# A mixture-of-experts stage on one core: shared expert with stationary weights over 512 tokens, router sigmoid from tanh and silu

## Chip, cores and metric

One core of one Trainium2 chip runs the whole program. The metric is the device time of one execution in microseconds; the kernel before has a median of 911.48 us over 3 runs (911.13 to 911.8).

## What is computed

Two layers over x of 2 x 2048 tokens by 256 channels: attention, a mixture of experts, a time-mixing layer with a scan, a channel-mixing layer. The part that matters here is the mixture of experts on the normalised rows (E = 8 experts, F = 192, top 2):

```python
logits = x @ W_gate_router
scores = jax.nn.sigmoid(logits.astype(jnp.float32))
_, sel = jax.lax.top_k(scores + expert_bias, TOP_K)
top_scores = jnp.take_along_axis(scores, sel, axis=1)
top_scores = top_scores / (top_scores.sum(-1, keepdims=True) + EPS)
shared = jax.nn.silu(x @ Wg_s) * (x @ Wu_s) @ Wd_s
...
out = shared.at[tok].add(routed)
```

All matrix products are made of three passes on values split into a high and a low part (high x high, high x low, low x high), so every operand is converted twice: a copy to the high part (ScalarE, ACT) and a subtraction for the low part (VectorE, DVE).

## The kernel before

The program runs in stages with a barrier after the first: attention (0 to 333 us of the span), then in one block the dense stage (335 to 477), the slots of the routed experts (477 to 632) and the two last layers. The change lies in the dense stage. It takes 8 groups G of 512 tokens (4 tiles of 128). For each group:

- `z_of`, `turn_z`, `h_of`: the rows are normalised (ACT), transposed on TensorE (PE) and scaled to `hf`, 256 channels x 512 tokens, by ACT.
- `logits`: 16 PE matmuls of 8 columns against the router (line 1620); `sigmoid` on ACT (line 1243); `choose` on DVE, 13 small instructions from `sel` (line 1382) to `both` (line 1395), which many semaphore links serialise; `count` on PE (lines 1638, 1640) ranks the tokens; `weigh` and `rank_of` on DVE give weights and row numbers; GpSimd (POOL) scatters the rows to DRAM (line 1148).
- `h_hi`, `h_lo`: the split of `hf` into `hh` and `hl`; `turn_h`, `h_back`: rows transposed back for the scatter.
- The shared expert by tiles of 128 tokens, n = 0 to 31: `up(n)` has the tokens stationary and the gate and up weights moving, 6 matmuls of 384 columns (lines 80 to 82); `silu` (line 1253) and `hidden` (lines 1427, 1428) make the product; `turn` transposes it (lines 1656, 1657), `ht_hi` and `ht_lo` split it (lines 1258, 1434, 1435), `shared_down` multiplies with the down weights, 5 matmuls of 256 columns (lines 1664 to 1668), and `add` adds the tile to x (line 1440).
- `up_weights`, `down_weights`, `low_up_weights`, `low_down_weights`: one routed expert's weights per group are loaded and split.

Each engine goes through an order written out by hand: the loop over G in the blocks of ACT (line 1270 on), DVE (line 1456 on) and PE (line 1680 on). The shared expert of group G-1 is interleaved with the routing of group G. ACT holds one table of functions at a time; sigmoid and silu each bring a table load per group.

After group 7 DVE computes from the counts where the slots of the routed experts lie (lines 1464 to 1506). `fill_at` releases SP's eight fills of the rows behind each expert (line 1071); `tabled`, the fills and the scatters release SP's loads of slots (line 1082), with which the next stage begins.

Of the kernel before, what the change touches and what calls it, by code (L numbers as in the profile page):

```python
# [28 lines left out]
ALU = mybir.AluOpType  # L29
# [11 lines left out]
GT = 4  # L41
# [755 lines left out]
def experts_time_and_channels(nc, k, d):  # L797
# [7 lines left out]
    N1 = GROUPS * GT  # L805
# [6 lines left out]
    with ExitStack() as ctx:  # L812
# [18 lines left out]
        iota_e, iota_i = sl("iota_e", [P, E]), sl("iota_i", [P, P + 32], U32)  # L831
        sig, sel = sl("sig", [P, GT, E]), sl("sel", [P, GT, E])
        best, place = sl("best", [P, GT, 8]), sl("place", [P, GT, 8], U32)
# [21 lines left out]

        late = sb("late", [P, B * KC * D + KC * P + B * D])
        there, order, mine = (late[:, i * E * TPE:(i + 1) * E * TPE].rearrange("p (t e) -> p t e", e=E) for i in range(3))
        spot = late[:, 3 * E * TPE:3 * E * TPE + E + TPE + 2 * E + TPE + 2 + 2 * SLOTS]
# [20 lines left out]
        spare = dense.enter_context(nc.sbuf_tensor("spare", [P, 6 * KC * GW], F32))  # L879
# [3 lines left out]
        raw_gu = part(0, 4 * KC * F).rearrange("p (r c n) -> p r c n", r=2, c=KC)  # L883
        raw_dn = part(2048, 4 * D).rearrange("p (r c n) -> p r c n", r=2, c=2)
        gated_dn = part(3072, 2 * B * D).rearrange("p (b c n) -> p b c n", b=B, c=2)
        z = part(4096, GT * D).rearrange("p (t n) -> p t n", t=GT)
        hf = part(5120, KC * GW).rearrange("p (c n) -> p c n", c=KC)
# [61 lines left out]
        tp, dp, lg, bk = (bank[:, i] for i in range(4, 8))  # L949
        wgu_in, wdn_in = ([sem(f"m_{n}_in{i}") for i in range(2)] for n in ("wgu", "wdn"))  # L950
# [5 lines left out]
                 "ranked hb_ready hb_done gu_ready silu_done hid_done ht_ready ht_hi ht_lo d_done x_added "  # L956
                 "fill_at filled spread slots_known tabled z_turned y_done tagged tokened named "
# [93 lines left out]
        def _(sp):  # L1051
# [11 lines left out]
            weights(0, d["wg_s"], d["wu_s"], d["wd_s"])  # L1063
# [37 lines left out]
        def _(pool):  # L1101
# [54 lines left out]
            pool.wait_ge(s["tabled"], 1)  # L1156
            for c in range(KC):
                last = g_.tensor_scalar_mul(lnb[:, c], plain[:], col(k, "ln_b", c))
# [38 lines left out]
        def _(act):  # L1197
# [36 lines left out]
            def h_hi(G):  # L1234
                act.wait_ge(s["h_f"], (G + 1) * KC)
                need(act, s["gu_ready"], (G - 1) * GT)
# [18 lines left out]
            def ht_hi(n):  # L1255
                act.wait_ge(s["ht_ready"], n + 1)
                need(act, s["d_done"], n - 1)
                a_.copy(hth[:, n % 2], tp[:, 0:2 * P]).then_inc(s["ht_hi"], 1)
# [6 lines left out]
            z_of(1)  # L1265
            sigmoid(0)
            up_weights(1, 0)
            down_weights(1, 0)
            h_back(0, 0)
            h_back(0, 1)  # L1270
            for G in range(1, GROUPS + 1):
                n = (G - 1) * GT
                if G < GROUPS:
                    h_of(G)
                silu(n)
                if G < GROUPS:
                    sigmoid(G)
                    h_hi(G)
                if n:
                    ht_hi(n - 1)  # L1280
                silu(n + 1)
                ht_hi(n)
                if G < GROUPS:
                    h_back(G, 0)
                if G + 1 < GROUPS:
                    z_of(G + 1)
                silu(n + 2)
                ht_hi(n + 1)
                if G < GROUPS:
                    h_back(G, 1)  # L1290
                silu(n + 3)
                ht_hi(n + 2)
                if G < GROUPS:
                    up_weights(G + 1, G)
                    down_weights(G + 1, G)
            ht_hi(N1 - 1)

            def slot_hi(p):
                act.wait_ge(s["z_turned"], of_pair(p)[-1] + 1)
                need(act, s["gu_ready"], N1 + 2 * p - 2 if p >= 2 else 0)  # L1300
                a_.copy(pair_of(hh, p), pair_in_bank(p)).then_inc(s["hi_h"], 1)

            def pair_ht_hi(p):
                w = len(of_pair(p))
                act.wait_ge(s["ht_ready"], N1 + p + 1)
                act.wait_ge(s["d_done"], N1 + 2 * p)
                a_.copy(hth[:, 0:w], tp[:, 0:w * 2 * P].rearrange("p (r f) -> p r f", r=w)).then_inc(s["ht_hi"], 1)

            def y_of(j):
                act.wait_ge(s["d_done"], N1 + j + 1)  # L1310
# [14 lines left out]
            for p in range(PAIRS + 1):  # L1325
# [4 lines left out]
                for j in of_pair(p):  # L1330
                    silu(N1 + j)
# [11 lines left out]
                if p == PAIRS - 1:  # L1343
                    edge_hi(act, 0)
                    act.wait_ge(s["gu_ready"], N1 + SLOTS)
# [6 lines left out]
        def _(v):  # L1352
# [20 lines left out]
            def h_lo(G):  # L1373
                need(v, s["gu_ready"], (G - 1) * GT)
# [47 lines left out]
            def hidden(n):  # L1422
                v.wait_ge(s["silu_done"], n + 1)
                need(v, s["ht_ready"], n - 1 if n < N1 else N1 + (n - N1) // 2)
# [6 lines left out]
            def ht_lo(n):  # L1431
                v.wait_ge(s["ht_hi"], n + 1)
                need(v, s["d_done"], n - 1)
                vec.tensor_tensor(htl[:, n % 2], tp[:, 0:P], hth[:, n % 2, 0:P], ALU.subtract)
# [1021 lines left out]
```

## Time and profile before

| | before |
|---|---|
| median of 3 runs | 911.48 us |
| the profiled execution | 915.1 us, of it 913.4 us span |
| PE busy over the span, mean granted clock | 838.2 us (92%), 0.958 |
| dense stage, from the first load to the first slot on PE | 335 to 477 us |
| busy from 402 to 416 us (14 us) | PE 12.09, DVE 11.66, ACT 10.43, POOL 7.20 us |

### The profile page before, as it was taken

The numbers are of one execution on the slowest core, as the hardware profiler recorded it, in microseconds if no ns is written. First come the engines' busy times: TensorE is split into PE (matmuls) and PEld (weight loads), VectorE is DVE, ScalarE is ACT, GpSimd is POOL, SyncE is SP. The second block draws the span as 40 slices with busy tenths as digits, with TensorE's granted clock in tenths as the row PEclk, the third lists the DMA queues.
The fourth block names the chain that finished last, engine by engine and source line by source line (L and its number), as shares of the span: only waits on it lengthen the run. The fifth ranks groups of instructions, "written<-read, shape, count | busy, mean of one in ns | idle before, by whom it ended". The sixth has DMA issues, their size and how long they took to land.

```text
span 913.4 us, 16937 instructions
## 1 busy us (share of the span) xinstructions
PE 838.2 (92%) x5115; PEld 748.6 (82%) x5115; DVE 653.9 (72%) x1917; ACT 474.4 (52%) x1006; POOL 378.7 (41%) x427
## 2 busy tenths in 40 slices
PE   7999999999999978888869999999789899988997
PEld 6879998988999867777749999999567788876776
DVE  3665677655567767787865675577677998878986
ACT  1544343243434348878625666466254344449883
POOL 2542200267000023555542444475678886323330
PEclk9899999989999987999988999999799999989999
DMA  9200000000000023433235445343411200000112
GB/s 304 106 1 2 1 1 1 1 1 1 1 1 1 1 56 114 122 106 122 79 118 148 133 117 172 95 125 119 127 47 47 92 2 1 1 1 24 47 47 70
DMA packets 48072, 58.31 MB, mean 64 GB/s; under 512 B 5616, under 2 KB 43121, under 8 KB 47985
## 3 DMA queue, kind: packets, MB, share of 16 engines
q1 hardware_dynamic: 39856, 38.85, 14.6%
q0 software_dynamic: 6480, 16.92, 5.1%
q10 hardware_dynamic: 1648, 1.46, 0.5%
q8 instruction: 45, 0.74, 0.3%
q14 instruction: 43, 0.34, 0.1%
HBM read 34.91 MB, written 23.22 MB: 64 GB/s over the span
## 4 chain that ended last, share of the span: by engine, by line
PE 31%; DVE 16%; issue 7%; ACT 4%; POOL 2%; SPq 1%; DMA 1%; DVEq 0%; ACTq 0%; POOLq 0%
PE bank L80 7%; PE bank L81 6%; PE bank L82 6%; PE bank L1721 2%; PE bank L1729 2%; PE bank L1620 1%; DVE xm L2110 1%; PE bank L1737 1%; DVE st L2046 1%; PE bank L1738 1%; PE bank L1741 1%; PE bank L1739 1%; PE bank L1740 1%; DVE hth L1435 1%; DMA row_tiles<-region 1%
## 5 line engine op out<-in xcount | busy, mean ns | idle before, releaser
L374 ACT CAST pth<-tp 128x512 fp32r<-128x512 f32 (+3 forms) x80 | 41.7, 525 | 128.8 <-PE tp L735 127.5
L1164 POOL DMA_INDIRECT results<-row_tiles,idu x71 | 70.0, 986 | 91.1 <-ACT row_tiles L1313 76.7
L1148 POOL DMA_INDIRECT region<-row_tiles,posu x64 | 66.3, 1036 | 59.8 <-DVE posu L1419 42.7
L559 DVE TENSOR_TENSOR ptl<-tp,pth 128x512 fp32r<-128x512 f32 (+3 forms) x80 | 48.3, 608 | 54.6 <-ACT pth L374 54.5
L80 PE MATMUL cx<-vh,pth 128*128 128x256 f32 x272 | 80.7, 297 | 1.4 <-DVE ptl L559 1.2
L82 PE MATMUL cx<-vh,ptl 128*128 128x256 f32 x272 | 76.9, 283 | 0.0
L81 PE MATMUL cx<-vl,pth 128*128 128x256 f32 x272 | 76.9, 283 | 0.0
L80 PE MATMUL sc<-hh,ph 128*128 128x512 f32 (+3 forms) x160 | 61.2, 382 | 0.3
L82 PE MATMUL sc<-hh,pl 128*128 128x512 f32 (+3 forms) x160 | 58.3, 364 | 0.0
L81 PE MATMUL sc<-hl,ph 128*128 128x512 f32 (+3 forms) x160 | 58.1, 363 | 0.0
L365 ACT ACTIVATE prob<-sc,nmx 128x512 f32<-128x512 f32 (+3 forms) x80 | 49.4, 628 | 14.0 <-DVE nmx L530 14.0
L1253 ACT ACTIVATE act_g<-bank 128x192 f32<-128x192 f32 x103 | 34.1, 331 | 41.4 <-PE bank L82 40.5
L80 PEld LDWEIGHTS cx<-vh,pth 128*128 128x128 f32 x272 | 51.8, 190 | 3.0 <-DVE ptl L559 2.3
L80 PE MATMUL bank<-h3h,weights 128*128 128x512 f32 x128 | 52.3, 408 | 1.2 <-DVE h3l L1030 1.2
L263 POOL TENSOR_SCALAR z<-x,mv,rstd 128x256 f32<-128x256 f32 x24 | 30.3, 1273 | 54.6 <-PE tp L623 53.9
L81 PEld LDWEIGHTS cx<-vl,pth 128*128 128x128 f32 x272 | 51.9, 191 | 0.7
L80 PE MATMUL bank<-guh,hh 128*128 x142 | 52.1, 367 | 0.0
L82 PEld LDWEIGHTS cx<-vh,ptl 128*128 128x128 f32 x272 | 51.8, 190 | 0.0
L82 PE MATMUL bank<-h3h,weights 128*128 128x512 f32 x128 | 51.6, 403 | 0.0
L81 PE MATMUL bank<-h3l,weights 128*128 128x512 f32 x128 | 51.4, 402 | 0.0
L735 PE MATMUL tp<-ident,prob 128*128 128x128 f32 x272 | 43.6, 276 | 5.9 <-ACT prob L365 5.9
L81 PE MATMUL bank<-gul,hh 128*128 x142 | 48.8, 344 | 0.0
(430 smaller groups left out, 2802.1 us busy)
## 6 DMA issues: line engine op xcount, KB each, us to landing
row_tiles<-region SPq DMA_DIRECT2D x71, 130.0 KB, 2.4
pairs_a<-results SPq DMA_DIRECT2D x10, 512.0 KB, 4.4
x<-in_x SPq DMA_DIRECT2D x8, 512.0 KB, 8.6
out<-x SPq DMA_DIRECT2D x8, 512.0 KB, 2.9
pairs_b<-results SPq DMA_DIRECT2D x6, 512.0 KB, 4.3
early<-in_wmod SPq DMA_DIRECT2D x1, 1536.0 KB, 7.9
spare<-in_wg SPq DMA_DIRECT2D x8, 192.0 KB
spare<-in_wu SPq DMA_DIRECT2D x8, 192.0 KB
```

The lines of the kernel that those rows point to most:

```text
L80: eng.matmul(out, lh, rh, start=first, stop=False)
L81: eng.matmul(out, lh, rl, start=False, stop=False)
L82: return eng.matmul(out, ll, rh, start=False, stop=last)
L263: g_.tensor_scalar(z[:, G % 2, j], k.x[:, t], mv[:, t, 0:1], rstd[:, t:t + 1], ALU.subtract, ALU.mult).then_inc(s["z_done"], 1)
L365: a_.activation(prob[:, u % 2, o:o + w], sc[:, score_bank(m), 0:w], ACT.Exp, bias=nmx[:, t:t + 1], scale=1.0 / 16, accum_out=rsc[:, t, ch: ...
L374: a_.copy(pth[:, m % 2, 0:w], tp[:, m % 2, 0:w]).then_inc(s["pt_hi"], 1)
L559: vec.tensor_tensor(ptl[:, m % 2, 0:w], tp[:, m % 2, 0:w], pth[:, m % 2, 0:w], ALU.subtract).then_inc(s["pt_lo"], 1)
L735: last = nc.tensor.transpose(tp[:, m % 2, j * P:(j + 1) * P], prob[:, UNIT_OF[m] % 2, a:a + P], k.ident[:])
L1148: g_.indirect_dma_start(region, bass.IndirectOffsetOnAxis(ap=posu[:, c, t:t + 1], axis=0), hb[:, G % HB, j], None).then_inc(scattered[G % ...
L1164: g_.indirect_dma_start(results, bass.IndirectOffsetOnAxis(ap=idu[:, j % 8:j % 8 + 1], axis=0), y[:, j % YR, 0:D], None, bounds_check=KS * ...
L1253: a_.activation(act_g[:, n % 2], gu[:, n % 2, 0:F], ACT.Silu).then_inc(s["silu_done"], 1)
L1721: last = nc.tensor.transpose(zp[:, 0, o:o + P], gt[:, j % GR, c * P:(c + 1) * P], k.ident[:])
```

## The change

The shared expert goes by groups. `up_shared(G, m)` has 128 columns of the weights stationary and 512 tokens moving, 6 matmuls each; the weights are laid out on the host as gate 0 to 127, up 0 to 127, then gate and up 128 to 191 together, so m = 0, 1, 2 give three banks with the hidden channels on partitions. No transposes of the product are left. `shared_down` takes two tiles at a time into the one bank `dp`, 10 matmuls, and `add` adds two tiles. The router's sigmoid is made of tanh (0.5 tanh(x/2) + 0.5) and, where relu(-0.5 - x) is above zero, silu(x)/x. The orders of ACT, DVE and PE are written anew.

On ACT:

```diff
             def sigmoid(G):
                 act.wait_ge(s["logits"], G + 1)
                 need(act, s["route"], G)
-                a_.activation(sig[:].rearrange("p t e -> p (t e)"), bk[:, 0:GT * E], ACT.Sigmoid).then_inc(s["sig_done"], 1)
+                a_.copy(flat(logit), bk[:, 0:GT * E])
+                a_.activation(flat(silu_l), bk[:, 0:GT * E], ACT.Silu)
+                a_.activation(flat(sel), bk[:, 0:GT * E], ACT.Relu, bias=k.mhalf[:, 0:1], scale=-1.0)
+                a_.activation(flat(sig), bk[:, 0:GT * E], ACT.Tanh, scale=0.5).then_inc(s["sig_done"], 1)
...
+            def gate_wide(G):
+                act.wait_ge(s["up_ready"], 3 * G + 1)
...
+                a_.activation(wide, up_bank[0], ACT.Silu).then_inc(s["gated"], 1)
+            def gate_narrow(G):
+                act.wait_ge(s["up_ready"], 3 * G + 2)
+                a_.activation(narrow[0:F - P], up_bank[2][0:F - P], ACT.Silu).then_inc(s["gated"], 1)
+            def hid_hi(G):
+                act.wait_ge(s["multiplied"], 2 * G + 1)
...
+                a_.copy(h2[0:F - P], narrow[0:F - P]).then_inc(s["hid_hi"], 1)
+                act.wait_ge(s["multiplied"], 2 * G + 2)
+                a_.copy(h1h, wide).then_inc(s["hid_hi"], 1)
...
+            for G in range(GROUPS):
+                sigmoid(G)
                 if G + 1 < GROUPS:
                     z_of(G + 1)
+                h_back(G, 0)
+                h_back(G, 1)
+                gate_wide(G)
+                up_weights(G + 1, G)
+                gate_narrow(G)
+                if G + 1 < GROUPS:
+                    h_of(G + 1)
+                hid_hi(G)
+                if G + 1 < GROUPS:
+                    h_hi(G + 1)
+                down_weights(G + 1, G)
```

On DVE (behind the loop stand the table of slots, `add(7, 0)`, `add(7, 1)` and the copies that set `tabled`):

```diff
             def choose(G):
                 v.wait_ge(s["sig_done"], G + 1)
+                vec.reciprocal(logit[:], logit[:])
+                c_.link(vec.tensor_scalar(sig[:], sig[:], 0.5, 0.5, ALU.mult, ALU.add))
+                c_.link(vec.tensor_tensor(silu_l[:], silu_l[:], logit[:], ALU.mult))
+                c_.link(vec.copy_predicated(sig[:], sel[:].bitcast(U32), silu_l[:]))
...
+            def multiply_narrow(G):
+                v.wait_ge(s["gated"], 2 * G + 2)
+                vec.tensor_tensor(narrow[0:F - P], narrow[0:F - P], up_bank[2][F - P:P], ALU.mult).then_inc(s["multiplied"], 1)
+            def multiply_wide(G):
+                v.wait_ge(s["up_ready"], 3 * G + 3)
+                vec.tensor_tensor(wide, wide, up_bank[1], ALU.mult).then_inc(s["multiplied"], 1)
+            def hid_lo(G):
+                v.wait_ge(s["hid_hi"], 2 * G + 1)
+                vec.tensor_tensor(h2[F - P:P], narrow[0:F - P], h2[0:F - P], ALU.subtract).then_inc(s["hid_lo"], 1)
+                v.wait_ge(s["hid_hi"], 2 * G + 2)
+                vec.tensor_tensor(h1l[:], wide, h1h, ALU.subtract).then_inc(s["hid_lo"], 1)
+            def add(G, i):
+                v.wait_ge(s["down_done"], 2 * G + i + 1)
...
+                vec.tensor_tensor(xt, xt, dp, ALU.add).then_inc(s["x_added"], 1)
...
+            for G in range(GROUPS):
+                choose(G)
+                if G:
+                    add(G - 1, 0)
+                weigh(G)
+                rank_of(G)
+                if G:
+                    add(G - 1, 1)
+                if G == GROUPS - 1:
                     v.wait_ge(s["const2"], 2)
                     c_.link(vec.tensor_copy(fillu[:], base[:]))
                     v.sem_inc(s["fill_at"], 1)
+                multiply_narrow(G)
+                multiply_wide(G)
+                low_up_weights(G + 1, G)
+                hid_lo(G)
+                if G + 1 < GROUPS:
+                    h_lo(G + 1)
+                low_down_weights(G + 1, G)
```

On PE:

```diff
+            def up_shared(G, m):
+                for c in range(KC):
+                    last = three(nc.tensor, up_bank[m], gsh[:, c, up_cols(m)], gsl[:, c, up_cols(m)], hh[G % 2][:, c], hl[G % 2][:, c],
+                                 c == 0, c == KC - 1)
+                last.then_inc(s["up_ready"], 1)
+            def shared_down(G, i):
+                pe.wait_ge(s["hid_lo"], 2 * G + 2)
+                need(pe, s["x_added"], 2 * G + i)
...
+            for G in range(GROUPS):
+                logits(G)
...
+                if G:
+                    shared_down(G - 1, 0)
+                turn_h(G, 0)
+                if G:
+                    shared_down(G - 1, 1)
+                turn_h(G, 1)
+                pe.wait_ge(s["lo_h"], (G + 1) * KC)
...
+                up_shared(G, 0)
...
+                count(G)
...
+                up_shared(G, 2)
+                if G + 1 < GROUPS:
+                    turn_z(G + 1)
+                need(pe, s["multiplied"], 2 * G)
+                up_shared(G, 1)
+            shared_down(GROUPS - 1, 0)
...
+            shared_down(GROUPS - 1, 1)
```

Before, PE and ACT also turned z of group 1 ahead of everything else of group 1; now `turn_z(1)` stands behind `up_shared(0, 2)`. The slots keep their work and count their semaphores from zero; buffers move.

## Rows read from the trace of the kernel before

**Rows 1.** The page: busy time, share of the span and instructions of each engine.

```profile
PE 838.2 (92%) x5115; PEld 748.6 (82%) x5115; DVE 653.9 (72%) x1917; ACT 474.4 (52%) x1006; POOL 378.7 (41%) x427
```

**Rows 2.** Timeline of PE, dense stage: start us, us, instruction, idle time and releaser.

```profile
422.08 0.60 PE L1632 MATMUL bank<-ident,spare 128*128 128x128 f32 x4
...
422.99 0.42 PE L80 MATMUL bank<-gsh,hh 128*128 128x384 f32 x1
...
425.52 0.36 PE L1664 MATMUL bank<-dsh,hth 128*128 128x256 f32 x1
...
426.20 1.04 PE L1612 MATMUL bank<-ident,spare 128*128 128x128 f32 x8
427.00 0.42 PE L80 MATMUL bank<-gsh,hh2b 128*128 128x384 f32 x1
...
428.54 1.95 PE L1620 MATMUL bank<-router,spare 128*128 128x8 f32 x16 [0.25 <-ACT spare L1231]
...
443.93 1.95 PE L1620 MATMUL bank<-router,spare 128*128 128x8 f32 x16 [0.25 <-ACT spare L1231]
```

**Rows 3.** Timeline of DVE, one group of the dense stage.

```profile
416.68 0.29 DVE L1434 TENSOR_TENSOR htl<-bank,hth 128x128 fp32r<-128x128 f32 x1 [2.15 <-issue]
...
417.64 0.18 DVE L1382 TENSOR_TENSOR sel<-sig,rows 128x32 f32<-128x32 f32 x1
...
419.83 0.27 DVE L1427 TENSOR_TENSOR hid<-act_g,bank 128x128 f32<-128x128 f32 x1
...
422.74 1.29 DVE L1377 TENSOR_TENSOR hl2b<-spare,hh2b 128x512 fp32r<-128x512 f32 x2
...
427.90 0.96 DVE L1360 TENSOR_TENSOR gul<-spare,guh 128x768 fp32r<-128x768 f32 x1
...
429.44 0.27 DVE L1427 TENSOR_TENSOR hid<-act_g,bank 128x128 f32<-128x128 f32 x1
```

**Rows 4.** Timeline of ACT, dense stage.

```profile
342.65 2.08 ACT L1220 ACTIVATE spare<-x,nmr,rstd 128x256 f32<-128x256 f32 x4
...
348.48 0.58 ACT L1248 COPY row_tiles<-bank 128x512 f32<-128x512 f32 x1 [1.01 <-PE bank L1632]
...
415.24 1.13 ACT L1238 CAST hh2b<-spare 128x512 fp32r<-128x512 f32 x2
...
416.66 1.28 ACT L1253 ACT_TABLE_LOAD   x1
```

**Rows 5.** Timeline of PE in the attention stage: matmuls of 512 columns, eleven in sequence.

```profile
305.22 0.39 PE L81 MATMUL sc<-hl,ph 128*128 128x512 f32 x1
...
307.51 0.39 PE L82 MATMUL sc<-hh,pl 128*128 128x512 f32 x1
```

**Rows 6.** The same timeline at the start of the dense stage: the router's matmuls of groups 0 and 1.

```profile
340.19 3.56 PE L1620 MATMUL bank<-router,spare 128*128 128x8 f32 x16 [0.96 <-ACT spare L1231]
...
352.00 3.56 PE L1620 MATMUL bank<-router,spare 128*128 128x8 f32 x16 [2.23 <-ACT spare L1231]
```

**Rows 7.** Timeline of DVE and SP at the end of the dense stage.

```profile
458.46 0.17 DVE L1419 CAST posu<-posf 128x8 uint32<-128x8 f32 x1
...
461.51 9.55 SPq L1071 DMA_DIRECT2D region<-zero  x8
473.27 14.10 SPq L1082 DMA_DIRECT2D row_tiles<-region  x9
...
479.02 0.69 DVE L1521 TENSOR_TENSOR hl<-bank,hh 128x512 fp32r<-128x512 f32 x1 [3.61 <-ACT hh L1301]
```

**Rows 8.** Busy by stretch, PE alone: us, PE busy (instructions), granted clock, DMA share, GB/s.

```profile
449.00:450.00 1.00, 1.00 (x6) 0.50 0.37 133
...
461.00:462.00 1.00, 0.00 (x0) 1.00 0.37 133
...
476.00:477.00 1.00, 0.00 (x0) 1.00 0.13 34
...
478.00:479.00 1.00, 0.37 (x2) 0.50 0.42 88
```

More of the change, by code:

```diff
@@ L1264, in _ @@
             down_weights(0, SH)
[L1265 to L1284, printed above, removed]
+            for G in range(GROUPS):
+                sigmoid(G)
                 if G + 1 < GROUPS:
                     z_of(G + 1)
[L1287 to L1296, printed above, removed]
+                h_back(G, 0)
[9 more added lines that the diff above has]
+                down_weights(G + 1, G)
             def slot_hi(p):
                 act.wait_ge(s["z_turned"], of_pair(p)[-1] + 1)
-                need(act, s["gu_ready"], N1 + 2 * p - 2 if p >= 2 else 0)
+                need(act, s["gu_ready"], 2 * p - 2 if p >= 2 else 0)
                 a_.copy(pair_of(hh, p), pair_in_bank(p)).then_inc(s["hi_h"], 1)
@@ L1330, in _ @@
                 for j in of_pair(p):
-                    silu(N1 + j)
+                    silu(j)
                 if 1 <= p < PAIRS - 1:
@@ L1453, in _ @@
             v.wait_ge(s["tokened"], 1)
-            choose(0)
-            weigh(0)
-            low_up_weights(1, 0)
-            low_down_weights(1, 0)
-            for G in range(1, GROUPS + 1):
-                n = (G - 1) * GT
-                if G == 1:
-                    rank_of(0)
-                if G == GROUPS:
+            for G in range(GROUPS):
[7 more added lines that the diff above has]
+                if G == GROUPS - 1:
                     v.wait_ge(s["const2"], 2)
@@ L1495, in _ @@
-                if G < GROUPS:
-                    weigh(G)
-                    h_lo(G)
-                hidden(n + 2)
-                ht_lo(n + 1)
-                add(n)
-                if G == GROUPS:
-                    v.wait_ge(s["slots_known"], 1)
-                    vec.tensor_copy(exf[:], lg[:, 0:SLOTS])
-                    vec.tensor_copy(exu[:], lg[:, 0:SLOTS])
-                    c_.link(vec.tensor_scalar(colf[:], lg[:, SLOTS:2 * SLOTS], -1.0, float(USED), ALU.mult, ALU.add))
-                    vec.tensor_copy(colu[:], colf[:]).then_inc(s["tabled"], 1)
@@ new lines, in _ @@
+                low_down_weights(G + 1, G)
+            c_.link(vec.tensor_tensor(n_e[:], base[:], ebase[:], ALU.subtract))
+            c_.link(vec.tensor_tensor(there, n_e[:].unsqueeze(1).to_broadcast([P, TPE, E]),
+                                      m128[:].unsqueeze(2).to_broadcast([P, TPE, E]), ALU.is_gt))
+            flat = lambda a: a.rearrange("p t e -> p (t e)")
+            c_.link(vec.tensor_tensor_scan(flat(order), plain[:, 0:1].to_broadcast([P, E * TPE]), flat(there), 0.0, ALU.mult, ALU.add))
@@ new lines, in _ @@
+            c_.link(vec.tensor_tensor(order, order, there, ALU.mult))
+            c_.link(vec.tensor_scalar(mine, order, own[:, 0:1], None, ALU.is_equal))
+            vec.tensor_reduce(in_e, mine.rearrange("p t e -> p e t"), AX.X, ALU.add)
+            c_.link(vec.tensor_reduce(in_t, mine, AX.X, ALU.add))
+            vec.tensor_tensor(terms[:, 0:E], in_e, iota_e[:], ALU.mult)
+            vec.tensor_tensor(terms[:, E:2 * E], in_e, by_e[:], ALU.mult)
+            c_.link(vec.tensor_tensor(terms[:, 2 * E:], in_t, by_t[:], ALU.mult))
@@ L1562, in _ @@
                 for j in of_pair(p):
-                    hidden(N1 + j)
+                    hidden(j)
                 if p == PAIRS - 1:
```

218 lines of the change are left out of this document (84 added, 134 removed).

## The prediction, made blind

> **What bounds the kernel now.** I read the page first: PE is busy 92% of the span and no other engine comes near [rows 1]. That is a mean over stages with different limits, so the stage that changes has to be read by itself, in the timelines of its engines. The router's matmuls mark the groups: they start at 428.54 and 443.93, so a group takes 15.39 us [rows 2]; from group 1 at 352.00 [rows 6] to group 7 at 443.93 it is 91.93 us for six, 15.32 each. Inside a group PE is not the limit. DVE waits 2.15 us once per group [rows 3], and the ACT timeline shows why: the low part of a tile waits for ACT's high part, and ACT goes through its queue of splits and Silu's table load of 1.28 us [rows 4]. So the period is a ring of waits from engine to engine, and removed work pays only where it lies on the ring that the new order makes. The chance to go wrong here is to add up the removed work.
>
> **What goes.** Per group the change removes from PE eight transposes; up falls from 24 matmuls of 384 columns to 18 of 512, which cost (307.51 - 305.22)/10 = 0.229 us each [rows 5]. From ACT go two table loads of 1.28, from DVE some 2 us in all (fewer, wider instructions, against four small ones more for the sigmoid). All of that is real, and I cost it at nothing: none of it sets the new period, as the next part shows. The cover is the ring itself.
>
> **The new ring.** PE's second `shared_down(G-1, 1)` waits for `add(G-1, 0)`, since both halves share one bank; on DVE that add stands behind `choose(G)`. On PE, everything that makes the next hidden product (`turn_h`, `up_shared` 0, `count`, `up_shared` 2, `turn_z`, `up_shared` 1) stands behind that `shared_down`. And on DVE, `choose(G+1)` stands behind `multiply_wide(G)`, which needs `up_shared` 1. So a DVE run and a PE run follow one another and do not overlap:
>
> DVE run, with 0.1 us off each duration because the next instruction starts that much earlier: `multiply_wide`, 512 columns from the matmul's bank, 0.69 [rows 7], taken 0.61. Low parts of a routed expert's weights, from 427.90 to 429.44: 1.54 [rows 3]. `hid_lo`, two of 512 columns, as the pair of `h_lo`, 1.29: taken 1.20; `h_lo` 1.20 [rows 3]. The four new small instructions of `choose`: the trace has none of their kind; from below four that hide behind each other, some 0.4, from above four linked ones as long as `sel`'s 0.18 [rows 3] with a link each, some 1.1; I take 0.8, nearer the linked end, since three of them carry links. The rest of `choose`, 417.64 to 419.83: 2.19 [rows 3]. `add` of 512 columns to its end: 0.69 [rows 7]. Sum 8.23.
>
> PE run: `shared_down` with ten matmuls; five with the lead of the first take 0.68, from 425.52 to 426.20 [rows 2], and five more 0.60: 1.28. `turn_h` and `count`, from 422.08 to 422.99: 0.91 [rows 2]. Three times six matmuls of 512 columns, 6 x 0.229 and 0.08 of lead: 1.45 each, 4.35. `turn_z`, 426.20 to 427.00: 0.80 [rows 2]. The last matmul's end, 0.39 less 0.23: 0.16 [rows 5]. Sum 7.50. Two hand-overs, an estimate of 0.2 together. **Ring at full clock: 8.23 + 7.50 + 0.2 = 15.93 us**, 0.6 more than 15.32.
>
> ACT stays off it: in the DVE run it has to deliver the high part of the wide product, `h_hi` (1.13 for the pair [rows 4]), the down weights and the four small functions, some 3.5 us ending before `choose` is reached, 4.6 us into the run. The routing's tail (`weigh`, `rank_of`, the second `add`) runs on DVE during the PE run, some 3.2 us of 7.5. SP's and POOL's queues keep their order and counts; a weight load has a whole group of slack.
>
> **The clock.** In the new order PE has only `logits`, ten matmuls and four transposes to do during the 8.2 us of the DVE run, and then stands for some 3.7 us until the add. Before, the group had no such hole and the router's matmuls ran at 1.95 [rows 2]. Two rows bear on it. At 461 to 462 PE did nothing and the granted clock stayed 1.00 [rows 8]; at 476 to 477 PE did nothing either, and by 478 to 479 it was 0.50; at 449 to 450, right behind a busy group, it was 0.50 with PE busy throughout [rows 8]. So the clock falls after thin work, not surely after one short hole. I expect it to fall in nearly every group and to come back within the PE run. The price: from below 0 (no fall), from above 7.5 (the whole run at half clock). The nearest rows are the same 16 matmuls at 3.56 [rows 6] and 1.95 [rows 2], 1.6 lost; some of the slow stretch lies in the wait, where it costs nothing, so I take 1.3. **Ring with it: 17.2 us.**
>
> The Trainium skill, "TensorE: Matmul & The Clock Gate", section "Why this matters for your kernels", says to leave no gaps between bursts of matmuls, or the clock goes back to its lower level. By that rule the fall comes in every group and the ring is 17.2; by the row at 461 alone it would not come and the ring is 15.93. No run here shows this order yet.
>
> **The start.** Group 0's logits end at 340.19 + 3.56 = 343.75 [rows 6]. Sigmoid with one table load, 1.9: 345.7. `z_of(1)` comes next on ACT, 2.0, then `h_back`, 0.58 [rows 4]: 348.25. `turn_h` at half clock 0.7, `up_shared` 0 at half clock 2.6: 351.5. From there at full clock `count` 0.56, `up_shared` 2 1.45, `turn_z` 0.80, `up_shared` 1 1.45: **group 1 starts at 355.8 instead of 352.00**, 3.8 later (at half clock to the end, 360.1). Before, group 1's z was turned while ACT and DVE worked at group 0's routing.
>
> **The end.** Group 7's logits start at 355.8 + 6 x 17.2 = 459.0, against 443.93: 15.1 later. Its row numbers came 458.63 - 443.93 = 14.7 after that [rows 7, 2]. Now: 0.1 and the DVE run 8.23, a hand-over 0.15, `shared_down` 1.28, `turn_h` 0.35, `up_shared` 1.45, `count` with its end 0.75, `rank_of` 1.0: 13.3, and 1.3 for the clock: 14.6. From there the fills led to the first slot load, 461.51 to 473.27 [rows 7]. They come up to 0.9 sooner, since an add of 0.61 stands ahead of `fill_at` where weights of 1.54 stood. But `tabled` now comes behind the whole product of group 7 and a PE round trip, 13 to 14 us after the row numbers, just where the fills' end is. I count 0.4 of the 0.9. Sum: 15.1 - 0.1 - 0.4 = **14.6 us later**. The later stages keep their time.
>
> The profiled execution took 915.1 us, 3.6 above the median of the three runs, 911.48. The difference is applied to the median: 911.5 + 14.6 = **926 us**; the profiled execution would be 929.7.
>
> **Rivals.** (A) The clock holds. For it: the idle microsecond at 461 and the steady groups of before. Against it: 478 and 449. Then the ring is 15.93: group 7 starts at 451.4, 7.5 later; row numbers 1.4 earlier relative to that; 0.4 off: 5.7, so 917 us. (B) Faster: the ring is not what I read, and what paces the groups is DVE's wait behind the table load, which goes. Its place is the 2.15 us before the low part [rows 3]; its price is a period of 15.39 - 2.15 = 13.24. Then 3.8 - 6 x 2.08 - 0.4 = -9.1: 902 us. It decides if DVE run and PE run together come under 15.0: 3.8 + 6 x (15.0 - 15.32) - 1.4 - 0.4 = 0. Against it: the wait on the add is written in PE's order, and every long term has its own row. (C) The change doesn't do what it says: tanh and silu do not share a table. Two loads of 1.28 per group remain. The one before tanh delays `choose` by about 0.1, as ACT had 1.1 us in hand; the one before the gate lies in ACT's wait. With 1.3 in group 0 that is some 2 us more than the forecast: 928 us.
>
> **How the numbers follow.** The forecast of 926 has a chance of 0.60, A 0.22, B 0.06, C 0.06; 0.06 is left for a ring near 15.0, where gain and loss cancel. Faster by over 0.2% (about what a measurement of this kernel can tell from no change): B and a little of the last, 0.07. Within 0.2%: 0.06. Slower: the rest, 0.87. The range reaches down to A less its unknowns, 917 - 3, and up to the forecast with about one more us of clock loss in each of the seven periods, 926 + 8: 914 to 934. The fully slow PE run and B lie outside.
>
> **What would show it.** Right: router matmuls 16 to 18.5 us apart; one wait of PE over 3 us per group, ended by the add; a DVE that hardly waits from `multiply_wide` to `add`; `up_shared` at 0.43 per matmul for part of most groups; no table load but the first; group 1 starting near 356. Wrong: a period under 15.0; PE's longest wait ended by something other than the add; the clock at 1.00 throughout (then A); a first slot load set by `tabled` by more than a microsecond; or later stages that change their own length.

## The result, and the profile after

The changed kernel takes **934.24 us** (median of four runs, 931.88 to 937.21), the kernel before on the same chip 911.64 (four runs). The ratio is 1.0239, with a 95% interval of 1.0193 to 1.0284: slower, by 22.6 us. The forecast was 926.0 with a range of 914 to 934, so the direction came out, the median lies 0.24 above the upper end, and the sum was 8 us short. The experiments below show whether the mechanism was the one forecast.

The profiled execution took 937.21 us with a span of 935.2, against 915.1 and 913.4 before. The page's busy times, to be read against [rows 1]:

```profile
PE 834.4 (89%) x5003; PEld 746.5 (80%) x5003; DVE 647.3 (69%) x1837; ACT 456.9 (49%) x983; POOL 378.1 (40%) x427
```

Every engine is busy for less time than before, and the span is 21.8 us longer. What grew is waiting, and the view of waits for the stretch from 360 to 486 us says of what (the columns are the sum in us, how often, and the longest):

```profile
PE bank L1670 <- DVE x L1465: 23.1, 7, 3.7
...
PE bank L1670 <- DVE h1l L1459: 9.8, 7, 1.5
```

L1670 is the first matmul of `shared_down`, L1465 the add, L1459 the second half of `hid_lo`. Seven times PE stands 3.3 us for the add, and seven times 1.4 us for the hidden product. Before, in the steady groups from 367 us on, PE's longest wait was 0.8 us, and ahead of the router's matmuls it was 0.25 [rows 2].

One group on DVE, in the timeline (start, duration, instruction, idle time before and its releaser):

```profile
414.85 0.69 DVE L1453 TENSOR_TENSOR spare<-spare,bank 128x512 f32<-128x512 f32 x1 [0.95 <-PE bank L82]
415.45 0.95 DVE L1372 TENSOR_TENSOR gul<-raw_up,guh 128x768 fp32r<-128x768 f32 x1
416.43 0.69 DVE L1457 TENSOR_TENSOR h2t<-spare,h2t 64x512 fp32r<-64x512 f32 x1
417.15 0.69 DVE L1459 TENSOR_TENSOR h1l<-spare,hth 128x512 fp32r<-128x512 f32 x1
417.76 1.29 DVE L1389 TENSOR_TENSOR hl<-spare,hh 128x512 fp32r<-128x512 f32 x2
...
419.63 0.34 DVE L1394 RECIPROCAL logit<-logit 128x32 f32<-128x32 f32 x1
...
420.69 0.19 DVE L1398 TENSOR_TENSOR sel<-sig,rows 128x32 f32<-128x32 f32 x1
...
422.64 0.68 DVE L1465 TENSOR_TENSOR x<-x,bank 128x512 f32<-128x512 f32 x1
```

Nothing after the first row shows an idle time: from `multiply_wide` (L1453) to the end of the add at 423.32 DVE works 8.47 us through. The four new small instructions of `choose` are the stretch from 419.63 to 420.69, 1.06 us here; in the eight groups they take 0.86 to 1.06, and the whole run takes 8.34 to 8.48 in the seven that end in such an add, 8.41 in the mean of the six periods. Then PE, in the same group:

```profile
423.46 0.36 PE L1670 MATMUL bank<-dsh,hth 128*128 128x256 f32 x1 [2.37 <-DVE x L1465]
...
424.48 0.42 PE L1672 MATMUL bank<-dsh,h1l 128*128 128x256 f32 x1
...
426.83 0.63 PE L82 MATMUL bank<-hh,gsl 128*128 128x512 f32 x1
427.25 0.57 PE L80 MATMUL bank<-hh,gsh 128*128 128x512 f32 x1
...
432.10 0.40 PE L82 MATMUL bank<-hh,gsl 128*128 128x512 f32 x1
```

The second `shared_down` starts 0.14 us after the add, and PE's run lasts from 423.46 to 432.50, 9.04 us. Its first 256-column matmuls come 0.12 apart, from 424.27 on they come 0.21 apart, and `up_shared` 0 goes at 0.43 a matmul until 427.7; from there on it is 0.23. That is the lower of the two clock levels (1.2 GHz) from 424.3 to 427.7. This group is not the usual one in one respect: its first `shared_down` ran slowly too. In the other six groups with two `shared_down` to do, the first ran at full speed, and the slow stretch of the matmuls lies on the second, behind the wait. The timeline of the group from 378.30:

```profile
382.36 0.28 PE L1671 MATMUL bank<-dsl,hth 128*128 128x256 f32 x1
382.48 0.28 PE L1672 MATMUL bank<-dsh,h1l 128*128 128x256 f32 x1
...
387.11 0.55 PE L1670 MATMUL bank<-dsh,hth 128*128 128x256 f32 x1 [3.69 <-DVE x L1465]
387.47 0.42 PE L1671 MATMUL bank<-dsl,hth 128*128 128x256 f32 x1
387.68 0.41 PE L1672 MATMUL bank<-dsh,h1l 128*128 128x256 f32 x1
```

The matmuls come 0.12 apart ahead of the wait and 0.21 behind it. In the six periods PE's run takes 8.85 to 10.21 us, 9.19 in the mean. The view by stretch gives the granted clock from one router group to the next (columns: us, then busy time and instructions of PE, PE's weight loads, DVE, ACT and POOL, granted clock, DMA share, GB/s):

```profile
342.60:360.80 18.20, 14.86 (x57) 12.83 (x57) 9.72 (x43) 11.37 (x21) 5.92 (x6) 0.54 0.29 88
360.80:378.30 17.50, 12.53 (x77) 11.28 (x75) 11.49 (x46) 9.06 (x21) 7.22 (x7) 0.90 0.28 91
...
414.70:432.30 17.60, 13.84 (x76) 12.42 (x76) 11.63 (x46) 9.42 (x21) 8.27 (x8) 0.81 0.31 99
...
467.40:483.60 16.20, 11.61 (x61) 10.39 (x61) 10.11 (x44) 5.45 (x13) 6.07 (x6) 0.68 0.16 58
```

Before, the four steady groups from 382.7 to 443.9 ran at 1.00. The router's matmuls now start at 342.55, 360.76, 378.30, 395.79, 414.65, 432.33, 449.90 and 467.36: 18.21 for group 0, then 17.77 as the mean of six, against 15.32 before [rows 2, 6].

With the row numbers (the end of the last `posu`, 483.61) and the first slot load (498.60) the difference of the two spans splits up:

| stretch | before, us | after, us | difference | forecast |
|---|---|---|---|---|
| up to group 0's logits | 340.19 | 342.55 | +2.4 | 0 |
| group 0 to group 1 | 11.81 | 18.21 | +6.4 | +3.8 |
| six periods | 91.93 | 106.60 | +14.7 | +11.3 |
| group 7's logits to its row numbers | 14.70 | 16.25 | +1.6 | -0.1 |
| row numbers to the first slot load | 14.64 | 14.99 | +0.3 | -0.4 |
| the rest | 440.1 | 436.6 | -3.5 | 0 |
| span | 913.4 | 935.2 | +21.8 | +14.6 |

The first and the last line are code that the change leaves alone, but for counts and places of buffers. In the ten traces of the changed kernel and of the experiments group 0's logits start anywhere between 336.10 and 343.65, and the rest after the first slot load takes 435.7 us in e1, 439.9 in e5 and 435.2 in e7, so these two differences are about the scatter of single executions.

### The profile page after: what moved, and what is told of

The parts are those of the page before. It is cut to its first block, busy times and chain, and to the rows that moved or that the text cites. A ratio compares the mean times of both kernels' runs of the same rounds, so it can differ in the third digit from the quotient of the medians.

```text
span 935.2 us, 16461 instructions
## 1 busy us (share of the span) xinstructions
PE 834.4 (89%) x5003; PEld 746.5 (80%) x5003; DVE 647.3 (69%) x1837; ACT 456.9 (49%) x983; POOL 378.1 (40%) x427
## 4 chain that ended last, share of the span: by engine, by line
PE 38%; DVE 16%; issue 5%; POOL 2%; ACT 2%; DMA 0%; SPq 0%; DVEq 0%; ACTq 0%; POOLq 0%
PE bank L80 8%; PE bank L81 8%; PE bank L82 8%; PE bank L1720 2%; PE bank L1728 2%; DVE xm L2109 1%; PE bank L1736 1%; PE bank L1616 1%; PE bank L1737 1%; PE bank L1740 1%; PE bank L1738 1%; PE bank L1739 1%; DVE st L2045 1%; PE bank L1636 1%; DVE gul L1372 1%
## 5 line engine op out<-in xcount | busy, mean ns | idle before, releaser
L82 PE MATMUL bank<-guh,hl 128*128 x142 | 48.8, 343 | 0.0
```

The costliest lines, as they stand in the source:

```text
L82: return eng.matmul(out, ll, rh, start=False, stop=last)
```

## The experiments

Two questions were open: is the ring of the prediction really what sets the pace, and what made it longer than 17.2? The periods of all kernels, worked out from the starts of the router's matmuls in one trace of each:

| kernel | group 1 starts | group 7 starts | mean of six periods | time, us | ratio to before |
|---|---|---|---|---|---|
| before | 352.00 | 443.93 | 15.32 | 911.64 | 1 |
| after | 360.76 | 467.36 | 17.77 | 934.24 | 1.0239 |
| e1 add first | 354.65 | 439.69 | 14.17 | 906.94 | 0.9949 (0.9910 to 0.9988) |
| e2 hole filled | 351.76 | 454.27 | 17.09 | 925.35 | 1.0170 (1.0119 to 1.0221) |
| e3 old sigmoid | 357.58 | 459.54 | 16.99 | 926.68 | 1.0163 (1.0125 to 1.0201) |
| e4 new sigmoid alone | 356.66 | 458.08 | 16.90 | 922.16 | 1.0106 (1.0059 to 1.0154) |
| e5 weights in the wait | 360.83 | 436.08 | 12.54 | 896.69 | 0.9825 (0.9789 to 0.9861) |
| e6 the same, old sigmoid | 357.54 | 438.79 | 13.54 | 902.16 | 0.9875 (0.9831 to 0.9920) |
| e7 start and tail | 351.54 | 429.48 | 12.99 | 893.59 | 0.9804 (0.9765 to 0.9842) |
| e8 Silu loads first | 356.91 | 433.10 | 12.70 | 897.07 | 0.9815 (0.9782 to 0.9848) |
| e9 swap alone | 352.01 | 451.37 | 16.56 | 922.84 | 1.0118 (1.0088 to 1.0147) |

**e1: the add ahead of `choose`.** One line of DVE's order moves.

```diff
-                choose(G)
                 if G:
                     add(G - 1, 0)
+                choose(G)
                 weigh(G)
```

> The changed kernel with one line moved on DVE: the first add of the group before stands ahead of choose instead of behind it. Theory (a ring of a DVE run and a PE run that cannot overlap because PE's second shared_down waits for the add behind choose): shared_down, turn_h and the first up_shared now run beside choose, so the PE run behind choose shrinks by about 1.3 + 0.35 + 1.45 = 3.1 us, the ring at full clock is near 13.3 us instead of 15.9, and the hole that let the clock fall closes; 7 periods of 17.8 become about 13.3 to 13.8, so 900 to 908 us, below the kernel before. Rival (the wait on the add is only where a slow DVE shows): DVE's work per group is unchanged, the period stays above 16 us and the time at 922 to 934.

Measured: 906.94 us, period 14.17 (13.95 from group 3 on). The time is inside what the theory expected, the period a little above it. Moving one instruction past `choose` takes 27 us off and turns the slower kernel into one that beats the kernel before by half a per cent. The other half of the expectation failed: the clock did not come back. It read 0.78 in the first of the six periods and 0.88 in every later one, so the gain does not come from the clock:

```profile
383.90:397.80 13.90, 12.49 (x76) 11.10 (x76) 11.61 (x46) 9.44 (x21) 7.98 (x8) 0.88 0.39 126
```

The timeline of DVE shows what the add waits for now:

```profile
417.47 0.69 DVE L1465 TENSOR_TENSOR x<-x,bank 128x512 f32<-128x512 f32 x1 [0.57 <-PE bank L1674]
418.07 0.35 DVE L1394 RECIPROCAL logit<-logit 128x32 f32<-128x32 f32 x1
```

DVE is early and waits 0.57 for the first `shared_down`; the small instructions follow the add instead of leading it.

**e2: the hole filled.** Fourteen matmuls of 512 columns, whose result nobody reads, stand on PE where it would wait for the add. The order of all real work stays.

```diff
                 turn_h(G, 0)
                 if G:
+                    pe.wait_ge(s["multiplied"], 2 * G)
+                    for i in range(14):
+                        nc.tensor.matmul(up_bank[1], gsh[:, i % 2, up_cols(1)], hh[(G - 1) % 2][:, i % 2], start=True, stop=True)
                     shared_down(G - 1, 1)
```

> The changed kernel with 14 matmuls of 512 columns more per group on PE, between turn_h and the second shared_down, into a bank that is free there and written anew later; nothing reads their result. They fill about 3.2 us of the wait for the add. Theory (ring of 15.9 to 16.1 at full clock, and 1.6 to 1.8 us per group lost to the half clock that follows the hole): the granted clock stays at 1.00 from group 2 on, the period goes from 17.8 to about 16.1, the time to 921 to 925 us though PE does more. Rival A (the clock is the whole loss): the period goes back to 15.4 or under and the time to 911 to 916. Rival B (the clock plays no part, the ring itself is that long): 934 us or more.

Measured: 925.35 us (922.86 to 931.09), 0.35 above what was expected. The period missed, 17.09 where 16.1 was expected, since the clock did not stay up from group 2 on. The interval of its ratio overlaps that of the changed kernel, so the reading rests on the groups of the trace and not on the two times. By stretch, two groups in sequence:

```profile
387.10:403.10 16.00, 14.27 (x91) 12.33 (x91) 11.51 (x46) 9.36 (x21) 7.98 (x8) 1.00 0.33 109
403.10:421.30 18.20, 16.83 (x91) 14.85 (x91) 11.64 (x46) 9.50 (x21) 8.26 (x8) 0.81 0.29 95
```

The first of them is what the run was for: with the clock at 1.00 from end to end the period is 16.00 (15.99 the other time it happened), and the ring at full clock was forecast at 15.93. PE still waits for the add there, 0.34 us, so the ring is what sets this period. Both rivals are out: 15.4 or under did not come, nor did 17.8 at full clock. The other four groups read 0.81 or 0.90. In the one from 403.07 the lower clock struck the fill itself, in PE's timeline:

```profile
406.32 0.58 PE L1670 MATMUL bank<-dsh,hth 128*128 128x256 f32 x1 [1.37 <-DVE h1l L1459]
...
409.32 4.89 PE L1690 MATMUL bank<-hh2b,gsh 128*128 128x512 f32 x14
414.05 0.28 PE L1670 MATMUL bank<-dsh,hth 128*128 128x256 f32 x1
```

Ahead of the fill PE still does thin work, the router's 8-column matmuls, and waits 1.37 for the hidden product. The clock fell in that wait (0.77 from 405 to 406, 0.50 behind it; the first `shared_down` goes at 0.21 a matmul). It came back inside the fill, between 412 and 413, so the fourteen matmuls took 4.89 us where they take 3.47 at full clock (from 391.96), and made the second `shared_down` late by themselves. The Trainium skill, "TensorE: Matmul & The Clock Gate", section "Why this matters for your kernels", asks for no idle gaps between bursts of matmuls. These rows agree that a filled gap can keep the clock up, in two of six groups, and they show that filling only the longer of two gaps is not enough.

**e3: the matmul half of the change alone.** The four activations and the four small DVE instructions go, one Sigmoid comes back.

```diff
-                a_.copy(flat(logit), bk[:, 0:GT * E])
-                a_.activation(flat(silu_l), bk[:, 0:GT * E], ACT.Silu)
-                a_.activation(flat(sel), bk[:, 0:GT * E], ACT.Relu, bias=k.mhalf[:, 0:1], scale=-1.0)
-                a_.activation(flat(sig), bk[:, 0:GT * E], ACT.Tanh, scale=0.5).then_inc(s["sig_done"], 1)
+                a_.activation(flat(sig), bk[:, 0:GT * E], ACT.Sigmoid).then_inc(s["sig_done"], 1)
...
-                vec.reciprocal(logit[:], logit[:])
-                c_.link(vec.tensor_scalar(sig[:], sig[:], 0.5, 0.5, ALU.mult, ALU.add))
-                c_.link(vec.tensor_tensor(silu_l[:], silu_l[:], logit[:], ALU.mult))
-                c_.link(vec.copy_predicated(sig[:], sel[:].bitcast(U32), silu_l[:]))
```

> The changed kernel with the router's sigmoid as before (one function, two table loads per group) and without the four small DVE instructions. Theory (the loads lie in ACT's waits, the four small ones lie on the ring): the period is 0.9 to 1.0 us shorter, less what the load of sigmoid delays choose, 0 to 0.3; the time 926 to 930 us, with 16 table loads in the stage. Rival (the loads were what paced the groups, so bringing them back costs): 1.3 to 2.6 us more per group, 943 to 955 us.

Measured: 926.68 us (926.45 to 926.87), 7.6 less than the whole change; the intervals of the two ratios just touch. The trace says the same at like clocks: a group that reads 0.90 takes 16.62 to 16.72 us here and 17.46 to 17.57 in the changed kernel, 0.84 less in the mean, near the 0.9 to 1.0 expected. Sixteen table loads of 1.28 us stand in the stage, two a group, where the changed kernel has one, and still it is faster: in this order the loads fall into ACT's waits while the small instructions stand on the ring. The sigmoid half, meant to save those loads, cost 7.6 us by the medians.

**e4: the sigmoid half alone**, in the kernel before (the same eight instructions as in e3, the other way round, on the kernel before).

> The kernel before with only the sigmoid made of tanh and silu. Rows of before show DVE waiting 2.15 us per group behind Silu's load. Theory: that wait goes, the four small instructions (0.9 us) come, so the period goes from 15.4 to 14.1 to 14.5 us and the time to 901 to 906 us. Rival (another wait takes its place at once): 909 to 916 us.

Measured: 922.16 us, slower by 10.3 than the 911.91 beside it. Both expectations are missed. The faster one rested on DVE's 2.15 us [rows 3] being a wait behind Silu's table load. The kernel before already says no. Its ACT timeline around that wait:

```profile
413.34 1.28 ACT L1243 ACT_TABLE_LOAD   x1
415.14 0.20 ACT L1243 ACTIVATE sig<-bank 128x32 f32<-128x32 f32 x1 [0.52 <-PE bank L1620]
415.24 1.13 ACT L1238 CAST hh2b<-spare 128x512 fp32r<-128x512 f32 x2
416.27 0.37 ACT L1258 CAST hth<-bank 128x256 fp32r<-128x256 f32 x1
```

The high part that DVE waits for is done at 416.64. Silu's load, at 416.66 [rows 4], comes behind it and cannot have held it. The load ahead of it is the Sigmoid's, and behind that load ACT still waits 0.52 for the logits, so this load was hidden. The timelines of DVE and ACT in one group of e4:

```profile
461.94 0.29 DVE L1443 TENSOR_TENSOR htl<-bank,hth 128x128 fp32r<-128x128 f32 x1 [2.49 <-ACT hth L1263]
```

```profile
460.07 0.18 ACT L1245 COPY logit<-bank 128x32 f32<-128x32 f32 x1 [1.82 <-PE bank L1629]
...
460.48 1.16 ACT L1239 CAST hh2b<-spare 128x512 fp32r<-128x512 f32 x2
461.51 0.40 ACT L1263 CAST hth<-bank 128x256 fp32r<-128x256 f32 x1
```

No load stands here any more, and DVE waits 2.49 us all the same. ACT's queue holds it: the sigmoid's copy waits 1.82 for the logits, and the high part that DVE needs stands behind it and behind the pair of `h_hi`. The load and the wait of before, 1.28 and 0.52, have become one wait of 1.82. What remains of the edit is 0.87 to 0.91 us more on `choose`, and a clock that no longer stays up: the stretches of four groups of e4 read 0.81, 1.00, 0.90 and 0.81, and the periods there 18.18, 16.33, 16.84 and 18.23. Even at 1.00 a group takes some 0.95 us more than before's 15.38 at 1.00, about the four instructions.

**e9: one swap, with the add left where the change put it.**

```diff
                 multiply_narrow(G)
+                low_up_weights(G + 1, G)
                 multiply_wide(G)
-                low_up_weights(G + 1, G)
                 hid_lo(G)
```

> The changed kernel with one swap: the low up weights (0.95 us) go ahead of multiply_wide, into VectorE's wait for up1; choose stays ahead of the add. Theory (the ring of the prediction: multiply_wide, low weights, hid_lo, h_lo, low_down, choose, add, and then PE's run): 0.95 less in each of seven groups, mean period from 17.77 to 16.8 (16.5 to 17.1) and 926 to 929 us. Rival (the pace of the changed kernel is PE's own work at a lowered clock, VectorE's list does not count): the period stays at 17.5 to 18.0 and the time at 933 to 936.

Measured: 922.84 us and a period of 16.56, so 1.21 less a group where the theory had 0.95, and the time is under its range; the rival is out. The DVE run, `multiply_wide` to the end of the add, takes 7.45 us in each of the six groups instead of 8.41 in the mean: 0.96 less, as the theory had it. The rest is the clock. In the views of waits and of lines DVE's wait for `up_shared` 1, which was 7.4 us in the changed kernel, is 0.6, and PE's wait for the add is down from 23.1 to 19.4, 0.53 a time:

```profile
PE bank L1670 <- DVE x L1465: 19.4, 7, 3.5
```

```profile
L1453 DVE TENSOR_TENSOR spare<-spare,bank 128x512 f32<-128x512 f32 x8 | 5.5, 688 | 0.6
```

One group, from 402.93, took 15.09 us, the 15.99 of e2 less 0.90. Its granted clock is 0.89, but there all of the slow stretch lies ahead of the wait, on the first `shared_down` and half of `turn_h`, and from 410.73 on PE runs at full clock: here the slow stretch cost nothing, because of where it fell.

**e5: both moves**, e1's order and e9's swap.

> The first experiment's order, and the low up weights (0.95 us) moved from behind multiply_wide to ahead of it, into the 0.95 us that VectorE waits there for up1. Theory (a ring through VectorE's order and the rest of PE's run sets the pace): the add comes 0.95 sooner in every group, the period falls from 13.95 to 13.0 (12.8 to 13.3), seven of them are 6.6: 898 to 903 us. Rival (the ring is already broken and PE's own work or the clock sets 13.95): the period stays at 13.7 to 14.1 and the time at 905 to 908.

Measured: 896.69 us, a bit under the expected 898, and 15 us under the kernel before. The period is 12.54, better than the 13.0 expected, because the clock now holds in four groups of six; the two others, at 0.87, take 13.1. By stretch:

```profile
373.10:386.20 13.10, 12.56 (x76) 11.15 (x76) 11.49 (x47) 9.38 (x21) 9.01 (x9) 0.87 0.41 131
386.20:398.50 12.30, 11.11 (x77) 9.87 (x77) 11.42 (x47) 9.43 (x21) 8.65 (x9) 1.00 0.46 143
```

In a group at 1.00 DVE is busy 11.4 of 12.3 us and PE 11.1: the two now work side by side, and DVE's own work leaves less than 1 us a group to gain from order.

**e6: e5 with the old Sigmoid** (e3's edit on top of e5).

> The same as the kernel with the weights in the wait, with the one Sigmoid of before in place of the four activations and four small VectorE instructions (the weight of the route is then the Sigmoid's own value). Theory: with the add ahead of choose the four small instructions (1.06 us) no longer stand between the up banks and the add, so they are off the ring, and the two table loads lie in ScalarE's waits: within 2 us of that kernel, 897 to 904. Rival (VectorE's busy time is now the bound): 1.06 a group less, 891 to 895. Second rival (ScalarE with the loads is too late with the hi part of the hidden values): slower by 3 to 10 us.

Measured: 902.16 us, with an interval that overlaps e5's, so the times don't settle it; the trace does. DVE has 0.7 us less to do a group, and the period at a clock of 1.00 is 13.2 instead of 12.25:

```profile
357.60:370.80 13.20, 11.20 (x78) 9.80 (x76) 10.66 (x42) 11.66 (x20) 7.75 (x8) 1.00 0.38 122
```

ACT's timeline in that group shows the reason:

```profile
360.66 1.28 ACT L1256 ACT_TABLE_LOAD   x1
361.95 0.20 ACT L1256 ACTIVATE sig<-bank 128x32 f32<-128x32 f32 x1
```

and the waits from 357.6 to 383.9 what follows from it:

```profile
PE bank L1629 <- ACT sig L1256: 1.6, 2, 0.8
```

The load stands right ahead of the Sigmoid, and the first half of `turn_h` (L1629 here) waits 0.8 us for the Sigmoid to have read the bank that it writes. The second half waits another 0.6 for the first `h_back`, which stands behind the Sigmoid and `z_of` in ACT's queue; in the group of e5 from 386.23 PE waits 0.67 in this place, for the add. So the second rival comes nearest, but not for the reason that it gave, the high part of the hidden values: in the short ring the load is on the path, and the tanh and silu form pays. The same form costs 7.6 us by the medians in the changed kernel's order and gains about 0.95 us a group in this one, where the clock is 1.00.

**e7 and e8: start and tail.** On top of e5: in group 0 the two `h_back` go ahead of `z_of(1)`, the last add goes behind the slot table, and a dummy activation ahead of group 0's logits is to load the table (a Tanh in e7, a Silu in e8).

```diff
+            a_.activation(act_g[:, 0, 0:GT * E], hf[:, 0, 0:GT * E], ACT.Tanh)
             for G in range(GROUPS):
                 sigmoid(G)
-                if G + 1 < GROUPS:
+                if 0 < G < GROUPS - 1:
                     z_of(G + 1)
                 h_back(G, 0)
                 h_back(G, 1)
+                if G == 0:
+                    z_of(1)
...
             add(GROUPS - 1, 0)
-            add(GROUPS - 1, 1)
             v.wait_ge(s["slots_known"], 1)
...
             vec.tensor_copy(colu[:], colf[:]).then_inc(s["tabled"], 1)
+            add(GROUPS - 1, 1)
```

> The kernel with the weights in the wait, with the start and the tail reordered: one dummy Tanh loads the table before the first logits (1.28 us off), in group 0 the two h_back go ahead of the normalising of group 1 (1.2 us off what up0 of group 0 waits for), and the last add moves behind the slot table. Theory for the start (ScalarE's load and its z_of delay up0 in group 0): from group 0's logits to group 1's 15.62 falls to 13.1 (12.8 to 13.6). Rival (the normalised group 1, now later, delays turn_z and up1): 14.6 to 15.6. Tail: row numbers' end to the gather's landing falls from 15.3 to 14.6, or stays if the scatter queue sets it. In all 3 us below that kernel: 895 to 900; with the rival, within 1 of it.

> The kernel with the reordered start and tail, with the dummy activation a Silu in place of a Tanh. The Tanh one brought no load with it, and the load of 1.28 us still stood between the copy of group 0's logits and the Silu (340.07). Theory: the table in place before holds tanh too but not silu, so a Silu ahead of the first logits moves the load there, where ScalarE waits 0.9 for them, and group 0's turn_h and up0 come about 1.28 earlier: from logits to logits 13.8 to 14.1 for group 0 in place of 15.25, and 0.9 to 1.4 us off the time (892.2 to 892.7, too little to be told from 893.6 by the times alone). Rival (the load only moves and the first Silu is as late, or another wait is behind it): 15.1 to 15.4.

Measured: e7 893.59 us, the fastest of all, e8 897.07; their intervals and e5's overlap, so the three can't be ranked; each is clearly faster than the kernel before. Both times lie outside their expectations, e7's under 895, e8's over 892.7. The tail did its part: row numbers to the first slot load took 13.8 us in e7 (439.99 to 453.77) and 14.9 in e5 (446.14 to 461.01). At the start e7 missed: 15.25 where 13.1 was expected. The number lies in the rival's range, but `turn_z` waits for nothing there, so the rival's reason is not the cause. Its ACT timeline shows what went wrong:

```profile
338.75 0.23 ACT L1294 ACTIVATE act_g<-spare 128x32 f32<-128x32 f32 x1
...
340.07 1.28 ACT L1257 ACT_TABLE_LOAD   x1
341.37 0.20 ACT L1257 ACTIVATE silu_l<-bank 128x32 f32<-128x32 f32 x1
```

The dummy Tanh brought no load and the Silu behind it did. In e8 the load came with the dummy Silu, and from the start of group 0's logits to `up_shared` 0 it took 7.15 us instead of 8.15: about the gain expected of it. Yet group 0 took 16.29 in all, missing theory and rival. PE's timeline of e8:

```profile
347.77 0.77 PE L80 MATMUL bank<-hh,gsh 128*128 128x512 f32 x1
...
353.68 0.63 PE L82 MATMUL bank<-hh,gsl 128*128 128x512 f32 x1
```

The lower clock lasted through `up_shared` 0 and 2, and what was won on ACT was lost there. In e7 it ended ahead of `up_shared` 2, at 347.8.

## Why the prediction was right, and where it was short

**The ring: right.** The forecast was 8.23 + 7.50 + 0.2 = 15.93 us at full clock; the two groups of e2 that kept the clock took 16.00 and 15.99. e1, e9 and e5 shorten it where the prediction said that it runs: `choose` off it gives -3.6 us, the low weights off it -1.2, both -5.2. The DVE run measured 8.41 in the mean instead of 8.23, PE's run 7.46 in e2's group at 1.00 instead of 7.50. Inside the DVE run some terms cancel: in the group from 414.85 the four new instructions took 1.06 instead of 0.8, `hid_lo` and the low weights 0.24 more than their terms, the rest of `choose` 1.95 instead of 2.19.

**The work taken away: rightly costed at nothing, for the table loads.** e3 and e4 show it from the other side: taking the loads away gained nothing in either order, since they lay in a wait there. For PE's transposes and narrower matmuls it is argued from PE's waits and was not tested by itself. The 2 us named for DVE came to some 0.7 a group (12.2 us busy before, 11.5 to 11.6 after). One reading of the prediction was wrong: the load that it names for DVE's wait, Silu's at 416.66 [rows 4], starts after the high part was done (416.64). The forecast did not rest on it, rival B and e4's expectation did.

**The clock: the term that was mis-sized.** "I take 1.3" measured 9.19 - 7.46 = 1.7 us a group, PE's run in the mean of six periods against the run at full clock. The reason given for taking less than the 1.6 lost by sixteen matmuls [rows 6, 2] was that some of the slow stretch lies in the wait. It seldom did: in six of the seven groups the matmuls of the first `shared_down` came 0.12 apart, and the slow ones are those of the second, of `turn_h` and, in most groups, of the start of `up_shared` 0, all behind the wait (387.11 above). The group of 423.46 has a slow stretch ahead of the wait as well (417.90 to 420.20), which cost nothing, and a second one behind it, which made PE's run 9.04. The dearest period, 18.86 from 395.79, is the one in which the clock was at 0.50 from 401 on, through the wait and to the end of `up_shared` 0. With the 0.2 more of the DVE run, six periods make +14.7 instead of +11.3.

**The start: the same error.** The step that failed is "From there at full clock `count` 0.56, `up_shared` 2 1.45". Timeline of PE:

```profile
354.95 0.77 PE L80 MATMUL bank<-hh,gsh 128*128 128x512 f32 x1
...
357.66 1.87 PE L1616 MATMUL bank<-ident,spare 128*128 128x128 f32 x8
359.22 0.55 PE L80 MATMUL bank<-hh,gsh 128*128 128x512 f32 x1
```

`up_shared` 2 at 354.95 and `turn_z` at 357.66 ran at the lower clock too; only `up_shared` 1 came at full clock. That is +6.4 instead of +3.8; the bound named for it, half clock to the end, was 360.1, and 360.76 came in an execution that was 2.4 later from the beginning.

**The end: the same error, and a wait foreseen too small.** Group 7's row numbers took 16.25 after its logits, not 14.6: its second `shared_down` and `up_shared` 0 ran at half clock (0.68 in the stretch above). `tabled` did set the first slot load: the last add waits for a `shared_down` that is itself behind the table's matmul.

```profile
496.50 0.69 DVE L1465 TENSOR_TENSOR x<-x,bank 128x512 f32<-128x512 f32 x1 [2.65 <-PE bank L1674]
...
497.64 0.20 DVE L1520 CAST colu<-colf 128x71 uint32<-128x71 f32 x1
```

That cost 0.35 where a gain of 0.4 was forecast; e7, with that add behind the table, is 1.1 us quicker there than e5. A slot load set by `tabled` by more than a microsecond was on the prediction's own list of signs of being wrong, and by this figure it came, for the tail alone.

**Rivals.** A, the clock holds, did not happen in this kernel. B, faster through the lost table load, fell in e4: the wait was not the load's, and DVE waits 2.49 us without it. C, two tables, is out: in the whole dense stage there is one load.

```profile
L1257 ACT ACT_TABLE_LOAD x1 | 1.3, 1283 | 0.0
```

Not settled is what makes the lower clock come in one group and not in the next. The slow stretches follow thin work and a wait on PE, but in e2 and e5 the clock holds in some groups and falls in others with the same instructions in every one.

## What to carry to other kernels

When a change merges small steps into wide ones, write down for each engine what stands behind what in its queue, and look for a chain that passes through two engines in turn; here the pace was one add behind `choose`, and moving it was worth 27 us, in a change that had cost 22.6 us with all the work that it removed. Put work that nobody waits for into an instruction's wait, as the low weights into the wait for `up_shared` 1. Before removing an operation that stands ahead of a wait, ask what the waiting engine would do in its place: the same table loads were hidden in two orders, and one of them was on the path in a third.

## What the runs showed of the hardware

- The granted clock fell in a wait of 1.37 us behind the router's 8-column matmuls (e2, 405 to 406: 0.77) and came back only inside the fourteen 512-column matmuls that followed (0.50 to 412, 0.82 from 412 to 413). In the group ahead, with the same instructions, it stayed at 1.00.
- At the lower level matmuls came 0.43 us apart at 512 columns and 0.21 at 256, at the higher one 0.23 and 0.12 (after, 423.46 to 432.10).
- Copy, Silu, Relu and Tanh ran 8 groups on one table load (after, 346.33). With the table in place ahead of the stage a Tanh ran without a load and a Silu did not (e7, 338.75 and 340.07; e8, 343.20).
- The same slow stretch can cost nothing or 1.5 us: PE's run of 7.46 us (e2, 395.77) took 9.04 where it fell behind the wait (after, 423.46), and 7.45 where it fell ahead of it (e9, 410.73).
- A reciprocal of 128x32 took 0.34 us on DVE, three times the 0.11 of the `tensor_scalar` of that shape behind it in e5.
